# Cross attention's row maxima from sums and differences of key pairs, in a decoder layer on one Trainium2 core

## The reference

```python
q = (query @ Wq + bq).reshape(b, sq, 16, 64)
k = (key @ Wk + bk).reshape(b, 1601, 16, 64)
v = (value @ Wv + bv).reshape(b, 1601, 16, 64)
scores = jnp.einsum('bqhd,bkhd->bhqk', q, k) / 8
attn = jax.nn.softmax(scores, axis=-1)
out = jnp.einsum('bhqk,bkhd->bqhd', attn, v).reshape(b, sq, 1024)
out = out @ Wo + bo + residual        # then a layer norm with gamma, beta
```

## Time and profile before

| | us |
|---|---|
| median of 3 runs | 1935.51 |
| lowest and highest run | 1913.4, 1937.34 |
| span of the profiled execution | 1916.1 |
| second sweep of each of the pairs 1 to 5 | 147.4 to 147.5 |
| second sweep of pair 0, with two first sweeps beside it | 195.7 |

### The profile page before, as it was taken

The page is one execution under the profiler, slowest core; times in us unless marked ns, Lnnn a source line. Parts: engine busy times, 40 slices in busy tenths (PEclk is TensorE's granted clock), DMA queues, the critical chain, the costliest instruction groups (busy, mean ns, idle before and its releaser), DMA issues.

```text
span 1916.1 us, 29762 instructions
## 1 busy us (share of the span) xinstructions
PE 1767.4 (92%) x10698; PEld 885.2 (46%) x10698; DVE 1270.0 (66%) x2503; ACT 920.3 (48%) x1866; POOL 940.8 (49%) x800
## 2 busy tenths in 40 slices
PE   7999989998988999999999999999999999999983
PEld 3544444443444544445545545544554554554431
DVE  5677777777643657756656655665665675667888
ACT  2345676666665243344454444445445444445441
POOL 1000000000001466658888888898888888882111
PEclk9867999999999899999999999999999999999996
DMA  4232113332011000000000000000000000000001
GB/s 115 34 37 35 21 16 36 36 45 55 2 34 55 11 0 1 1 11 4 1 11 4 1 10 4 1 11 1 4 11 1 4 1 1 4 11 23 1 28 38
DMA packets 29129, 34.48 MB, mean 18 GB/s; under 512 B 4290, under 2 KB 27139, under 8 KB 27523
## 3 DMA queue, kind: packets, MB, share of 16 engines
q1 hardware_dynamic: 28984, 32.59, 9.1%
HBM read 14.99 MB, written 4.19 MB: 10 GB/s over the span
## 4 chain that ended last, share of the span: by engine, by line
PE 76%; DVE 16%; ACT 4%; issue 3%; SPq 1%; DMA 1%; POOL 0%; ACTq 0%; DVEq 0%; POOLq 0%
PE psum L974 17%; PE psum L954 14%; PE psum L939 9%; DVE maxima L1247 8%; PE psum L860 8%; PE psum L772 6%; PE psum L810 4%; PE psum L835 4%; PE psum L1005 3%; PE psum L927 3%; PE psum L872 2%; PE psum L986 2%; DVE parts_room L1341 1%; DVE stack_room L1297 1%; ACT stack_room L1116 1%
## 5 line engine op out<-in xcount | busy, mean ns | idle before, releaser
L1247 DVE TENSOR_REDUCE maxima<-psum 128x1 f32<-128x400 f32 (+5 forms) x1664 | 860.1, 580 | 322.7 <-PE psum L939 211.7
L747 POOL TENSOR_TENSOR parts_room<-parts_room,weights_room 128x512 f32<-128x512 f32 (+1 forms) x565 | 706.1, 1283 | 136.3 <-ACT weights_room L1137 136.3
L1137 ACT ACTIVATE weights_room<-psum 128x512 f32<-128x512 f32 (+1 forms) x757 | 405.5, 599 | 491.2 <-PE psum L954 429.4
L1065 ACT ACTIVATE weights_room<-psum 128x512 f32<-128x512 f32 (+3 forms) x640 | 300.2, 535 | 183.4 <-PE psum L835 104.1
L1455 POOL TENSOR_SCALAR rstd<-meanvar 128x2 f32<-128x2 f32 (+1 forms) x24 | 9.8, 408 | 726.9 <-DVE meanvar L1197 726.9
L954 PE MATMUL psum<-stack_room,dk_hi 64*128 64x512 f32 (+1 forms) x1408 | 264.1, 410 | 8.1 <-ACT weights_room L1137 4.8
L939 PE MATMUL psum<-k_later,stack_room 64*128 64x400 f32 (+1 forms) x896 | 243.4, 412 | 22.3 <-DVE stack_room L1297 14.6
L939 PEld LDWEIGHTS psum<-k_later,stack_room 64*128 64x128 f32 x896 | 128.4, 184 | 220.8 <-issue 121.2
L974 PE MATMUL psum<-weights_room,parts_room 128*64 128x512 f32 (+1 forms) x754 | 203.1, 606 | 0.0
L974 PE MATMUL psum<-weights_room,late_room 128*64 128x512 f32 (+1 forms) x760 | 202.5, 605 | 0.0
L835 PE MATMUL psum<-stack_room,stack_room 51*128 51x512 f32 (+3 forms) x640 | 143.4, 448 | 34.2 <-DVE maxima L1247 31.7
(11 more groups left out here) (136 smaller groups left out, 1854.4 us busy)
## 6 DMA issues: line engine op xcount, KB each, us to landing
stack_room<-parts_room SPq DMA_DIRECT2D x84, 128.0 KB
x_block<-x_dram SPq DMA_DIRECT2D x8, 512.0 KB, 4.8
x_middle<-x_block SPq DMA_DIRECT2D x4, 512.0 KB, 3.1
x_block<-x_middle SPq DMA_DIRECT2D x4, 512.0 KB, 3.9
out_dram<-x_block SPq DMA_DIRECT2D x8, 256.0 KB, 2.1
stack_room<-parts_room SPq DMA_DIRECT2D x24, 64.0 KB
parts_room<-ctx_dram SPq DMA_DIRECT2D x1, 1536.0 KB
stack_room<-shift_rows SPq DMA_DIRECT2D x64, 2.0 KB
```

The lines of the kernel that those rows point to most:

```text
L747: engine.tensor_tensor(sum_[:kw, :], old[:kw, :], weights[u % NP_WEIGHTS][:kw, :], ALU.add) \
L1065: engine.activation(w_self[s % NW][:, m, 0:n], bank_of(use + m)[:, 0:n], ACT.Exp, scale=SELF_SCALE).then_inc(emptied(use + m), 1)
L1137: engine.activation(weights[u % NP_WEIGHTS][:kw, :], pair_scores[u % NSCORES][:kw, :], ACT.Exp, scale=CROSS_SCALE).then_inc(pair_exp, 1)
L1247: engine.tensor_reduce(maxima[:, p % 2, i // TB, n, i % TB, ch:ch + 1], bank_of(use + n)[:, 0:real - k0], AX.X, ALU.max) \
```

## The change

The keys are paired, key j with key j + 799, for j from 0 to 801 (1602 places for 1601 keys, so one key stands in two pairs). For two scores a and b, the larger is (a + b) / 2 + |a - b| / 2. The keys' sums and differences are made once for a pair of heads, and a matmul with the queries gives a + b and a - b. A query tile still has four chunks of 400, 402 columns: difference, sum, difference, sum (`CROSS_CHUNKS` now says which). ACT reads the two banks of a difference chunk and writes their sizes to SBUF. DVE reads the sum chunk from PSUM and the sizes from SBUF in one instruction, that adds them, halves, and takes the maximum along the row. The room for the sizes are the two x blocks, which are idle in that stretch.

```diff
+KEY_PAIRS = SE // 4 * 2 + 2
+KEY_SHIFT = S - KEY_PAIRS
+PAIR_HALF = KEY_PAIRS // 4 * 2
+CROSS_CHUNKS = [(apart, n, (0, PAIR_HALF, KEY_PAIRS)[n], (0, PAIR_HALF, KEY_PAIRS)[n + 1])
+                for n in range(2) for apart in (True, False)]
...
-        return steps + [(0, lambda kind=kind, b=b: self.put(kind, p, b))
-                        for kind, b in (("key_steps", NK - 1), ("key_rests", NK - 2), ("key_rests", NK - 1))]
+        return steps + [(0, lambda kind=kind, b=b: self.put(kind, p, *b))
+                        for kind, b in (("key_steps", (NK - 1,)), ("key_pairs", ()), ("key_rests", (NK - 2,)),
+                                        ("key_rests", (NK - 1,)))]
...
+    apart_sizes = [x_blocks[n // 2][:, n % 2 * HT:(n % 2 + 1) * HT, :].rearrange("p t d -> p (t d)") for n in range(4)]
...
             elif kind == "pair_chunk":
                 p, i, ch = at
-                k0, k1, _ = CROSS_CHUNKS[ch]
+                apart_, _, k0, k1 = CROSS_CHUNKS[ch]
                 pe.wait_ge(*bank_read(use_of["project_queries", p, i // TB]))
-                for n in range(NK):
-                    pe.wait_ge(*bank_read(use_of["project_keys", p, n]))
-                pe.wait_ge(shifts_cleared, 1)
+                pe.wait_ge(key_pairs_made, p + 1)
                 for n in range(HP):
                     slot, r = take_bank(use + n), n * DH2
                     filled(use + n, engine.matmul(slot[:, 0:k1 - k0], q_hi[p % 2][r:r + DH2, i * P:(i + 1) * P],
-                                                  k_high(p)[r:r + DH2, k0:k1], start=True, stop=True))
+                                                  key_pairs(p)[r:r + DH2, int(apart_), k0:k1], start=True,
+                                                  stop=True))
...
                     if p:
                         act.wait_ge(keys_split, NK * p)
-                    if p >= 2:
-                        act.wait_ge(*bank_filled(use_of["pair_chunk", p - 1, NT - 1, len(CROSS_CHUNKS) - 1] + HP - 1))
-                    targets = [(k_whole[:, k0:k1], k1 - k0)] + [(k0_hi[p % 2], APART)] * (b == 0) \
-                        + [(k_high(p)[:, k0:k1], k1 - k0)]
+                        act.wait_ge(key_pairs_made, p)
+                    targets = [(k_whole[:, k0:k1], k1 - k0)] + [(k0_hi[p % 2], APART)] * (b == 0)
...
+            elif kind == "pair_chunk" and CROSS_CHUNKS[at[2]][0]:
+                p, i, ch = at
+                _, half, k0, k1 = CROSS_CHUNKS[ch]
+                no = key_halves_no[p, i, half]
+                for n in range(HP):
+                    act.wait_ge(*bank_filled(use + n))
+                    if no < 2:
+                        act.wait_ge(normed, 2 * NB)
+                        act.wait_ge(middle_out[no], 32)
+                    else:
+                        act.wait_ge(*bank_read(chunk_use(*key_halves[no - 2], False) + n))
+                    engine.activation(apart_size(p, i, half, n)[:, 0:k1 - k0], bank_of(use + n)[:, 0:k1 - k0], ACT.Abs) \
+                        .then_inc(emptied(use + n), 1)
...
+            elif kind == "pair_chunk" and not CROSS_CHUNKS[at[2]][0]:
+                p, i, ch = at
+                _, half, k0, k1 = CROSS_CHUNKS[ch]
+                for n in range(HP):
+                    dve.wait_ge(*bank_filled(use + n))
+                    dve.wait_ge(*bank_read(chunk_use(p, i, half, True) + n))
+                    size = apart_size(p, i, half, n)[:, 0:k1 - k0]
+                    engine.tensor_tensor_reduce(size, bank_of(use + n)[:, 0:k1 - k0], size, 0.5, LOWEST, ALU.add,
+                                                ALU.max, maxima[:, p % 2, i // TB, n, i % TB, half:half + 1]) \
                         .then_inc(emptied(use + n), 1)
                 newest_max = use + HP - 1
...
+            elif kind == "key_pairs":
+                p, = at
+                dve.wait_ge(keys_copied, NK * (p + 1))
+                if p >= 2:
+                    dve.wait_ge(*bank_filled(use_of["pair_chunk", p - 1, NT - 1, len(CROSS_CHUNKS) - 1] + HP - 1))
+                one, other = k_whole[:, 0:KEY_PAIRS], k_whole[:, KEY_SHIFT:S]
+                engine.tensor_tensor(key_pairs(p)[:, 0, :], one, other, ALU.add)
+                engine.tensor_tensor(key_pairs(p)[:, 1, :], one, other, ALU.subtract).then_inc(key_pairs_made, 1)
...
-                for k in (k_first, k_later):
-                    chain.on(engine.memset(k[:, S:SE].bitcast(F32), 0.0))
-                    after_last()
...
                 sp.wait_ge(normed, 2 * NB)
+                for n in range(HP):
+                    sp.wait_ge(*bank_read(chunk_use(*key_halves[-1], False) + n))
```

More of the change, by code:

```diff
@@ L56 @@
 SELF_SCALE, CROSS_SCALE = 1.0 / DH1 ** 0.5, 1.0 / DH2 ** 0.5
-QUARTER = (SE // 4) // 2 * 2
-CROSS_CHUNKS = [(k0, min(SE, k0 + QUARTER) if k0 < 3 * QUARTER else SE, min(S, k0 + QUARTER) if k0 < 3 * QUARTER else S)
-                for k0 in range(0, 4 * QUARTER, QUARTER)]
+KEY_PAIRS = SE // 4 * 2 + 2
[3 more added lines that the diff above has]
+                for n in range(2) for apart in (True, False)]
 KEY_BLOCKS = [(k0, min(S, k0 + BQ)) for k0 in range(0, S, BQ)]
@@ L501, in _decoder @@
     pair_step_of = {a[:3]: a[3] for a in pair_scores_at}
+    key_halves = [(p, i, CROSS_CHUNKS[ch][1]) for p, i, ch in (s.at for s in stages if s.kind == "pair_chunk")
+                  if CROSS_CHUNKS[ch][0]]
+    key_halves_no = {a: n for n, a in enumerate(key_halves)}
     steps_done = {a[:3]: n + 1 for n, a in enumerate(s.at for s in stages if s.kind == "pair_values")}
@@ L670, in _decoder @@
     late_room = Room(nc, sb, "late_room", NS * P * 4)
-    k_first, k_later = late_room.take([SE], F32R), sb("k_later", [P, SE], F32R)[:, :]
+    pairs_first = late_room.take([2, KEY_PAIRS], F32R)
+    pairs_later = sb("pairs_later", [P, 2, KEY_PAIRS], F32R)[:, :, :]
     v_pair = [v_pair0, late_room.empty().take([NS, P], F32)]
@@ L689, in _decoder, with key_pairs, apart_size, chunk_use @@
                         for n in ((0, 1), (2, 3)))
-    def k_high(p):
-        return k_later if p else k_first
+    def key_pairs(p):
+        return pairs_later if p else pairs_first
+    apart_sizes = [x_blocks[n // 2][:, n % 2 * HT:(n % 2 + 1) * HT, :].rearrange("p t d -> p (t d)") for n in range(4)]
+    def apart_size(p, i, half, n):
+        return apart_sizes[(key_halves_no[p, i, half] * HP + n) % 4]
+    def chunk_use(p, i, half, apart):
+        return use_of["pair_chunk", p, i, 2 * half + (not apart)]
     def apart(b):
@@ L1240, in vector_program @@
                     .then_inc(emptied(use), 1)
-            elif kind in ("chunk", "pair_chunk"):
+            elif kind == "chunk":
                 p, i, ch = at
-                k0, *_, real = self_chunks(i)[ch] if kind == "chunk" else CROSS_CHUNKS[ch]
+                k0, k1 = self_chunks(i)[ch]
                 dve.wait_ge(consts_set, ALL_CONSTS)
@@ L1259, in vector_program @@
                     dve.wait_ge(*bank_filled(use_of[rows, was, b]))
-                engine.tensor_reduce(shift[:, p % 2, b, :],
-                                     maxima[:, p % 2, b, :, :, :].rearrange("p n t c -> p (n t) c"), AX.X,
+                found = maxima[:, p % 2, b, :, :, :].rearrange("p n t c -> p (n t) c")
+                engine.tensor_reduce(shift[:, p % 2, b, :], found if kind == "negate" else found[:, :, 0:2], AX.X,
                                      ALU.max, negate=True).then_inc(shift_ready, 1)
```

6 lines of the change are left out of this document (5 added, 1 removed).

## The result

| | before | after |
|---|---|---|
| median of 20 runs each, us | 1925.62 | 1938.47 |
| lowest and highest run | 1903.64, 1939.43 | 1928.9, 1958.72 |
| span of the profiled execution | 1916.1 | 1930.4 |

What follows compares the result with a forecast made beforehand. PE was taken to bound the steady pairs, DVE's reading to pace pair 0 and the block alone. 28.8 + 4 + 1 - 3.5 + 0 = +30 us on 1916.1 gives 1946; with 19.4 added, 1966 us, range 1918 to 2012.

Steps and rivals of the forecast that it cites:

- The main term: Steady pairs, order scores, difference, scores, sum chunk: Abs queues behind two exponentials; eight 0.60 us stalls a pair, +28.8 us.
- S comes out as before: Steady pairs, other stage orders: the sum chunk (S) after a difference chunk keeps its earlier timing; 0.
- the faster rival: Both readers work side by side, Abs never stands behind exponentials, PE's stalls go: 1877 us; chance 0.12.
- the combined instruction's +4 us: Steady pairs: writing DVE's maximum adds 0.08 us at nine places a pair; +4 us, bounds 0 and 31.
- Key pairs: Making key sums and differences on DVE before the chunks, hidden in idle time: +1 us, bounds 0 and 12.
- Pair 0: First pair, 48 more chunk stages: gains between back-to-back chunks against delays behind scores; 0, bounds -14 and +8.
- the block alone: The block whose chunks run alone: 0.35 to 0.40 us a bank in place of 0.48; -3.5 us.
- The baseline: Whole kernel: the median of the runs lies 19.4 us above the profiled span of 1916.1 us.
- Absorbed: The delays occur, but PE regains them at later bank waits and pair 0 gives some back: about 1940 us; chance 0.18.
- The slow instruction: DVE's combined instruction takes 1.0 to 1.14 us: 2008 us; chance 0.14.
- The clock: Steady pairs: more holes on PE lower its clock to 0.97, 27 us more, 1993 us; chance 0.07.
- The tables: Abs makes ACT reload its tables, 64 switches a pair: 2122 us or above; chance 0.02.

Runs made afterwards that it cites:

- abs_ahead: Changed kernel, with ACT taking the Abs before the preceding scores' exponentials at nine places a pair (eleven in pair 0): 1907.88 us, ratio 0.9911.
- short_reduce: Kernel before the change, with cross attention chunk reductions reading 340 of 400 columns: 1906.04 us in one run, steady pair 144.2 us.
- no_maximum: Changed kernel, with DVE only adding sum chunk and sizes and taking no maximum: 1950.84 us in one run, steady pair 151.0 us.
- the second profile of after: The changed kernel itself, unaltered, measured again: 1943.58 us against 1924.83, ratio 1.0113, pair 0 199.4 us.
- ahead_warm: abs_ahead, plus two idle 128x512 PE matmuls a chunk stage in the block whose chunks run alone: 1913.87 us, ratio 0.9945.
- neither warm kernel: ahead_warm, and one with a 256-column idle matmul a stage there, on abs_ahead's order widened to 21 places a pair: 1913.87 and 1901.81 us.
- abs_later: Changed kernel, with the Abs at the same nine places also behind the next scores' exponentials: 2028.02 us in two runs, ratio 1.0558.
- the memset: Changed kernel, with POOL writing zeros in place of its subtraction for the low part of the keys: one run, steady pair 151.1 us.

## Why the prediction was right or wrong

**The main term: right in kind, and each stall right in size.** The timeline of the cycle that answers to the earlier trace rows, per engine (start us, us):

```profile
1160.29 0.45 PE L958 MATMUL psum<-pairs_later,stack_room 64*128 64x400 f32 x2
...
1163.40 0.65 PE L1006 MATMUL psum<-parts_room,ones_v 128*64 128x512 f32 x2
```
```profile
1163.00 0.18 PEld L958 LDWEIGHTS psum<-pairs_later,stack_room 64*128 64x128 f32 x1 [0.83 <-ACT x_block L1153]
```
```profile
1160.77 0.57 DVE L1289 CUSTOM_DVE_ANT_0 x_block<-psum,x_block 128x400 f32<-128x400 f32 x1 [1.55 <-PE psum L958]
1161.27 0.08 DVE L1289 DVE_READ_ACCUMULATOR2_ANT maxima<- 128x1 f32 x1
1161.27 0.57 DVE L1289 CUSTOM_DVE_ANT_0 x_block<-psum,x_block 128x400 f32<-128x400 f32 x1
```
```profile
1161.47 1.09 ACT L1168 ACTIVATE weights_room<-psum 128x512 f32<-128x512 f32 x2 [3.97 <-PE psum L974]
1162.44 0.91 ACT L1153 ACTIVATE x_block<-psum 128x402 f32<-128x402 f32 x2
```

Count from the cycle's first chunk matmul. Before, the weight load for S's second head came at 1163.05 - 1160.97 = 2.08 us and the softmax sums at 2.57. After, they come at 2.71 and 3.11 us. That is 0.63 and 0.54 later, where 0.62 and 0.5 were forecast. The Abs stands behind the two exponentials, as replayed. The waits of pair 3 (total us, times, longest) give the count:

```profile
PEld psum L958 <- ACT x_block L1153: 6.5, 8, 0.8
...
PE psum L958 <- ACT x_block L1153: 3.4, 8, 0.5
PEld psum L958 <- DVE maxima L1289: 3.1, 17, 0.2
```

Eight waits a pair, none above 0.8 us, as said (the list has the figure nine times; at eight of them PE waited). Taking the stalls away gave 5.8 us a pair; the forecast for this term was 4.8, so it was 6.0 us too small over six pairs.

**First step that failed: "S comes out as before" in the other figures.** It was a gain set to 0. abs_ahead, with the stalls gone, stands at 145.3 us, 2.1 below before, 12.6 over six pairs. The prediction saw the 0.06 us by which an Abs ends sooner and let it go, because PE's waits for its reader seemed small. The last row above shows the waits for DVE halved, 6.8 us in 32 waits before, 3.1 in 17 after, and abs_ahead has the same 3.1 with none for an Abs beside them; short_reduce shows what such hundredths are worth. This is the term that was mis-sized most: it takes 12.6 off the +30. In the faster rival it had been counted, but together with the stalls' absence. They are separate: abs_ahead has the gain without the stalls, and after has both.

**Second step that failed: the combined instruction's +4 us.** The durations were forecast well: 0.573 us and a read of the accumulator of 0.083, together 0.65. But the read starts together with the next instruction (both at 1161.27 above), 0.07 us before its own instruction has ended, and ends 0.01 us after it: 0.58 us for the two, not 0.65. The timeline has PE's load into the bank of the combined instruction that ends at 1161.34:

```profile
1161.41 0.18 PEld L958 LDWEIGHTS psum<-pairs_later,stack_room 64*128 64x128 f32 x1 [0.18 <-DVE maxima L1289]
```
```profile
L1289 DVE CUSTOM_DVE_ANT_0 x_block<-psum,x_block 128x400 f32<-128x400 f32 x256 | 136.7, 572 | 199.0 <-PE psum L958 172.4 <-ACT x_block L1153 26.6
...
L1289 DVE DVE_READ_ACCUMULATOR2_ANT maxima<- 128x1 f32 x512 | 42.6, 83 | 0.0
```

That load started 0.07 us behind the main instruction's end. Whether the bank goes back with the main instruction or with the read can't be told from ends 0.01 us apart; no_maximum, without the read, gained 0.1 us a pair. The term is 0 to 0.6 us in six pairs. The Trainium skill's rule ("VectorE: DVE Perf Modes", section Two Vector instructions with no wait between them), that such an operation is two instructions, agrees with these rows; what was made of it here, that the second adds its 0.08 us to the time the bank is held, does not.

**Key pairs, +1 forecast: 0.** They are slower than forecast and hidden all the same. By shape, over all pairs but the first, and the timeline of pair 3 beside the earlier trace rows:

```profile
L1362 DVE TENSOR_TENSOR pairs_later<-parts_room 128x802 fp32r<-128x802 f32 x7 | 13.4, 1910 | 0.0
...
L1361 DVE TENSOR_TENSOR pairs_later<-parts_room 128x802 fp32r<-128x802 f32 x7 | 6.9, 986 | 0.0
```
```profile
1152.34 0.98 DVE L1361 TENSOR_TENSOR pairs_later<-parts_room 128x802 fp32r<-128x802 f32 x1
1153.24 1.88 DVE L1362 TENSOR_TENSOR pairs_later<-parts_room 128x802 fp32r<-128x802 f32 x1
1155.32 0.75 DVE L1339 SCALAR_TENSOR_TENSOR stack_room<-psum,parts_room,stack_room 128x512 fp32r<-128x512 f32 x1 [0.20 <-ACT stack_room L1134]
```

The second ends at 1155.12, and L1339, the split of the queries that the chunks wait for, then waits 0.20 us more for ACT. It starts 10.6 us into the pair's window, before 10.7. The cover had 0.2 us left: it held, but hardly.

**Pair 0 and the block alone.** Pair 0: 0 forecast, -1.4 measured, and +3.7 in the second profile of after, at clocks of 0.99 and 0.96 against 0.97, so not even its sign is known. The block alone: -3.5 forecast, -0.95 measured. TensorE's granted clock is 0.50 there, the 1.2 GHz level, and the turn of the ring was worked out from a bank filled 0.49 us after the matmul's start, a number from the full clock. ACT's timeline in it:

```profile
632.98 1.08 ACT L1153 ACTIVATE x_block<-psum 128x402 f32<-128x402 f32 x2 [0.79 <-PE psum L958]
634.85 1.08 ACT L1153 ACTIVATE x_block<-psum 128x400 f32<-128x400 f32 x2 [0.79 <-PE psum L958]
```

Four banks go by in 1.87 us, 0.467 each, where 0.35 to 0.40 was forecast, and ACT stands 0.79 us of it for PE. The window of before had shown the clock of 0.50; it was read and not used. The trace gives the chain of such a turn. A chunk matmul starts at 635.19 and an idle DVE begins on its bank at 635.93, 0.74 us later; in ahead_warm, at full clock in the same block, it is 0.49. DVE's second combined instruction starts 0.50 us behind its first and lasts 0.57, and the next matmul follows 0.06 later: 0.74 + 0.50 + 0.57 + 0.06 = 1.87 us. With 0.49 for the 0.74 it would be 1.62, an estimate that gives 0.405 a bank and 2.0 of the 2.55 us that are missing; the rest is DVE's 0.50, which the forecast had left out of the turn. No run showed the block so, as neither warm kernel had it at full clock with its own work alone.

**Sum.** Forecast 28.8 + 4 + 1 - 3.5 + 0 = 30. Measured, term by term: stalls 6 x 5.8 = +34.8, the earlier return of banks 6 x -2.1 = -12.6, combined instruction and key pairs 0, block alone -0.95, pair 0 -1.4: +20. The ratio of 1.010 is +19 us; the medians of all runs are 12.9 apart.

**The baseline.** 19.4 us were added for the distance of the profiled span to the median of three runs. With twenty runs that distance is 9.5, and in after 8.1. This is the largest single part of the 27.5 us, 11.3; the self attention's 6.2 in after's profile and some 10 from the terms make up the rest. Two of the three runs happened to lie high in a spread of 36 us (1903.64 to 1939.43), of the size of what the clock of the unchanged self attention does (23.7 us among the profiles).

**The rivals.** Faster did not happen. abs_ahead meets its condition, no chunk waiting for an Abs behind exponentials, and is 16 us below before (1907.88 to 1923.49), not 58. Absorbed fell with abs_later. The slow instruction fell (0.573 us). The clock stayed at 1.00 in after's steady pairs and moved only with the larger holes of abs_later. The tables were loaded no more often than before.

## What to carry to other kernels

When work moves to an engine with time to spare, look at what stands ahead of it in that engine's order: 0.5 us instructions that give a scarce buffer back belong ahead of those whose result is due only a cycle later. Where PE waits often and briefly (here 32 times 0.2 us a pair) for a short ring, count each hundredth of the reader's time as a gain or a loss. And take a baseline from windows of unchanged stretches, not from the median of three runs.

## What the runs showed of the hardware

- The granted clock of one and the same code differs from execution to execution: 0.87 to 0.94 over the self attention, which moved its end by 23.7 us (606.9 to 630.6), more than the whole change. The steady pairs at 1.00 repeat to 0.1 us.
- An elementwise DVE instruction with two SBUF inputs and a POOL instruction that reads SBUF hold each other up. DVE's second key pair instruction took a mean of 1.91 us where its twin took 0.99, and POOL's subtraction of 128x512 a mean of 1.645 us where it took 1.092 before:

```profile
L1528 POOL TENSOR_TENSOR dk_lo<-parts_room,dk_hi 128x512 fp32r<-128x512 f32 x16 | 26.0, 1645 | 5.0 <-ACT dk_hi L1140 5.0
```
```profile
1152.68 3.65 POOL L1528 TENSOR_TENSOR dk_lo<-parts_room,dk_hi 128x512 fp32r<-128x512 f32 x3 [0.76 <-ACT dk_hi L1140]
```

  The Trainium skill ("SBUF — State Buffer", section Who interferes with whom) has the later of the two block until the first is done, and a POOL instruction that only writes not contend. The trace agrees, turn by turn, in pair 3: DVE's first (1152.34, 0.98 us) is not slowed, POOL's subtraction that starts during it takes 1.59, DVE's second that starts during that takes 1.88, and POOL's next 1.84. With the memset DVE's second takes 0.98 to 0.99 in seven of eight pairs.
- Reading out an accumulator on DVE took 0.083 us, began with the next instruction and ended 0.005 to 0.011 us after its own, so it added 0.01 us and not 0.08.
- From the start of a chunk matmul of 400 columns to the start of an idle reader of its bank it took 0.74 us at a granted clock of 0.50 and 0.49 at 1.00.
